# Alibi attention stacks: one 72-row transfer each for queries and keys, with the bf16 parts stored singly

## What is computed

```python
q = (x @ Wq + bq).reshape(Bb, Ss, H, HD)      # H = 16, HD = 8
k = (x @ Wk + bk).reshape(Bb, Ss, H, HD)
v = (x @ Wv + bv).reshape(Bb, Ss, H, HD)
scores = jnp.einsum('bthd,bshd->bhts', q, k) / jnp.sqrt(jnp.asarray(HD, x.dtype))
alibi = _alibi_bias(Ss, Ss, x.dtype)          # slope of the head times -|k - q|
scores = scores + alibi[None]
scores = jnp.where(causal[None, None], -jnp.inf, scores)
attn = jax.nn.softmax(scores, axis=-1)
out = jnp.einsum('bhts,bshd->bthd', attn, v).reshape(Bb, Ss, Dd)
return out @ Wo + bo
```

## Time and profile before

| | |
|---|---|
| median of the runs | 1447.83 us |
| the profiled execution | 1447.86 us |
| its span, first to last instruction | 1446.1 us |
| PE busy | 1324.8 us, 92% |
| DVE busy | 1028.3 us, 71% |
| ACT busy | 754.1 us, 52% |
| POOL busy | 379.0 us, 26% |
| block C, first to last score matmul | 718.2 to 999.7 us |
| DMA data moved | 34.17 MB |

### The profile page before, as it was taken

How to read it: one execution, slowest core, us unless ns; L and a number is a source line. 1 busy time by engine, 2 the same in 40 slices (tenths; PEclk the granted TensorE clock), 3 DMA queues, 4 the chain that set the end, 5 groups by cost and what they waited for, 6 DMA issues and landing times.

```text
span 1446.1 us, 23967 instructions
## 1 busy us (share of the span) xinstructions
PE 1324.8 (92%) x9009; PEld 791.1 (55%) x9009; DVE 1028.3 (71%) x2201; ACT 754.1 (52%) x1617; POOL 379.0 (26%) x304
## 2 busy tenths in 40 slices
PE   6999999999999999999768999999889989899986
PEld 4777676767677766333222333334356765367652
DVE  5767776676857684776657676767578885898855
ACT  3545444444534443434224666666667874388851
POOL 0000000001000001334550000001458881498822
PEclk9999999999999999999866999999999999999998
DMA  5000000000000000000202321110011110011101
GB/s 147 1 1 0 1 1 1 1 1 1 1 1 1 1 1 0 1 1 0 96 19 81 90 80 39 39 37 2 23 27 31 31 32 8 4 39 31 31 15 30
DMA packets 28686, 34.17 MB, mean 24 GB/s; under 512 B 6594, under 2 KB 21132, under 8 KB 27276
## 3 DMA queue, kind: packets, MB, share of 16 engines
q1 hardware_dynamic: 28572, 32.64, 8.3%
HBM read 20.11 MB, written 4.39 MB: 17 GB/s over the span
## 4 chain that ended last, share of the span: by engine, by line
PE 74%; DVE 13%; ACT 4%; issue 3%; POOL 3%; DMA 2%; SPq 0%; POOLq 0%; DVEq 0%; ACTq 0%
PE ps L695 13%; PE ps L715 8%; PE ps L730 7%; PE ps L1067 5%; PE ps L1026 4%; PE ps L1047 3%; PE ps L1124 3%; DVE negmax L1459 2%; PE ps L904 2%; PE ps L898 2%; PE ps L666 2%; PE ps L1167 2%; PE ps L1250 2%; PE ps L1189 2%; PE ps L1221 2%
## 5 line engine op out<-in xcount | busy, mean ns | idle before, releaser
L2281 ACT ACTIVATE probsT<-ps 128x512 f32<-128x512 f32 (+1 forms) x304 | 163.8, 577 | 107.4 <-PE ps L1051 95.1
L1459 DVE TENSOR_REDUCE negmax<-ps 128x1 f32<-128x1024 f32 x128 | 150.7, 1219 | 72.6 <-PE ps L715 72.5
L2103 ACT ACTIVATE probs<-ps,negmax 128x1024 f32<-128x1024 f32 x128 | 142.5, 1114 | 80.6 <-DVE negmax L1459 76.7
L2456 POOL TENSOR_SCALAR rstd<-mv 128x4 f32<-128x4 f32 (+1 forms) x31 | 7.2, 232 | 595.9 <-DVE mv L1394 595.6
L2109 ACT COPY probsT<-ps 128x512 f32<-128x512 f32 x128 | 74.8, 584 | 168.2 <-PE ps L730 168.1
L730 PEld LDWEIGHTS ps<-ident,probs 128*128 128x128 f32 x1024 | 114.5, 141 | 66.3 <-issue 44.1
L730 PE MATMUL ps<-ident,probs 128*128 128x128 f32 x1024 | 138.2, 277 | 6.6 <-DVE probsT L1472 3.4
L1026 PE MATMUL ps<-arena 76*128 76x512 bf16 (+3 forms) x384 | 113.6, 355 | 26.6 <-DVE cmax L1727 20.8
L715 PE MATMUL ps<-k_st,q_st 64*128 64x512 f32 x512 | 128.8, 622 | 5.9 <-ACT probs L2103 5.9
L1727 DVE CUSTOM_DVE_ANT_0 k_st<-ps,rel 128x256 f32<-128x256 f32 (+7 forms) x128 | 96.8, 756 | 44.2 <-PE ps L1026 43.3
L1727 DVE CUSTOM_DVE_ANT_0 q_st<-ps,rel 128x256 f32<-128x256 f32 (+7 forms) x128 | 96.7, 756 | 42.0 <-PE ps L1026 41.2
(11 more groups left out here) (233 smaller groups left out, 2543.9 us busy)
## 6 DMA issues: line engine op xcount, KB each, us to landing
probsT<-probsT SPq DMA_DIRECT2D x62, 128.0 KB, 2.4
arena<-c_parts SPq DMA_DIRECT2D x32, 192.0 KB
arena<-c_parts SPq DMA_DIRECT2D x16, 128.0 KB
arena<-in_L_ffn_w_dram SPq DMA_DIRECT2D x3, 512.0 KB
c_parts<-probsT SPq DMA_DIRECT2D x2, 768.0 KB, 3.5
arena<-in_c_far_dram SPq DMA_DIRECT2D x16, 96.0 KB
c_parts<-work SPq DMA_DIRECT2D x2, 768.0 KB, 11.1
work<-in_L_ffn_wqkv_dram SPq DMA_DIRECT2D x1, 1536.0 KB, 11.9
```

What stands on the lines that cost most here:

```text
L1459: dve.tensor_reduce(negmax[:, u:u + 1], s2, AX_X, ALU.max, negate=True).then_inc(s_a_negmax, 1)
L2103: act.activation(probs[:, u % NPB, :], s2, ACT.Exp, bias=negmax[:, u:u + 1], accum_out=rowsum[:, u:u + 1]).then_inc(s_a_exp, 1)
L2281: act.activation(c_p[:, kt % 2, j0:j0 + heads, q0 - kt * P:q0 - kt * P + n], ps[:, 4 + c % 2, 0:heads * n].rearrange("p (h n) -> p h n", n ...
```

## The change

- The parts of queries and keys get a DRAM tensor each: `q_scr` of shape (batch, group, 3 parts, 32 rows, 1024) and `k_scr` of shape (batch, group, 5 slots, 32 rows, 1024), where slots 3 and 4 repeat parts 0 and 1.
- Each part is stored as soon as it is there, queries and keys apart: eight transfers of 256 KB per batch (3 for queries, 5 for keys) in place of two of 768 KB. The DRAM side of each starts with the 4 groups.
- A stack has nine products (also q2 with k2): its middle part is 72 rows on either side, and each side comes in one transfer. `SHALLOW` becomes 84 and `DEEP` 87.
- The constants of a stack (`c_far`) are a function of their own. For sequences 0 and 1 they are loaded once the weights of block B have been turned (`s_fp`), ahead of the stores; for the others they stay where they were, ahead of `c_stack`.
- PE waits for 5 transfers per stack (`STACK`) and not 9.

```diff
-SHALLOW = FAR + 64
+SHALLOW = FAR + 72
...
-        scr = nc.dram_tensor("c_parts", (2, 3, BATCH, P, SEQ), BF16, kind="Internal").ap()
+        q_scr = nc.dram_tensor("c_q_parts", (BATCH, GROUPS, 3, STRIP, SEQ), BF16, kind="Internal").ap()
+        k_scr = nc.dram_tensor("c_k_parts", (BATCH, GROUPS, 5, STRIP, SEQ), BF16, kind="Internal").ap()
...
-        STACK = 16 * 9
+        STACK = 16 * 5
...
-            def c_store(b):
-
-                for w in range(2):
-                    sp.wait_ge(s_c_r2, 2 * b + w + 1)
-                    sp.dma_start(scr[w, :, b, :, :].rearrange("n p c -> p n c"), c_part[b][:, w, :, :])\
-                      .then_inc(s_c_scr, 16)
+            def c_store(b, part):
+
+                sp.dma_start(q_scr[b, :, part], c_part[b][:, 0, part, :]).then_inc(s_c_scr, 16)
+
+            def c_store_keys(b, part):
+
+                for slot in range(part, 5, 3):
+                    sp.dma_start(k_scr[b, :, slot], c_part[b][:, 1, part, :]).then_inc(s_c_scr, 16)
+
+            def c_stores(b):
+
+                for part, done in enumerate((s_c_p0, s_c_p1, s_c_r2)):
+                    sp.wait_ge(done, 2 * b + 1)
+                    c_store(b, part)
+                    sp.wait_ge(done, 2 * b + 2)
+                    c_store_keys(b, part)
+                sp.wait_ge(s_c_scr, 16 * 8 * (b + 1))
...
+            def c_stack(s):
+
+                g, b, buf = s % GROUPS, s // GROUPS, s % 3
+                n = 4 * SEQ
+                q = q_scr[b, g].rearrange("t (e j) n -> (t e) (j n)", j=4)
+                k = k_scr[b, g].rearrange("t (e j) n -> (t e) (j n)", j=4)
+                k = bass.AP(k.tensor, k.offset, [[HD1 * n, 3], [n, 3 * HD1], [1, n]])
+                sp.dma_start(c_q2[buf][FAR:SHALLOW, :, :].rearrange("p j n -> p (j n)"),
+                             q.unsqueeze(0).to_broadcast([3, 3 * HD1, n])).then_inc(s_c_stack[buf], 16)
+                sp.dma_start(c_k2[buf][FAR:SHALLOW, :, :].rearrange("p j n -> p (j n)"), k)                  .then_inc(s_c_stack[buf], 16)
+
+            sp.wait_ge(s_fp, 9)
+            c_far(0)
+            c_far(1)
+            c_stores(0)
             c_stack(0)
             c_stack(1)
...
                 if s == 0:
                     sp.wait_ge(s_e_x2, UNITS_B)
+                    c_far(2)
                     c_stack(2)
-                    c_store(1)
-                    sp.wait_ge(s_c_scr, 64)
+                    c_stores(1)
                 if 1 <= s and s + 2 < SEQS:
                     sp.wait_ge(s_c_turned, NPARTS * s)
+                    c_far(s + 2)
                     c_stack(s + 2)
```

More of the change, by code:

```diff
@@ L513, in c_stack, with c_far @@
+            def c_far(s):
+                g, buf = s % GROUPS, s % 3
+                sp.dma_start(c_q2[buf][0:FAR, :, :].bitcast(U16), a["c_far"][0, g, 0:FAR]).then_inc(s_c_stack[buf], 16)
+                sp.dma_start(c_k2[buf][0:FAR, :, :].bitcast(U16), a["c_far"][1, g, 0:FAR]).then_inc(s_c_stack[buf], 16)
+                sp.dma_start(c_k2[buf][SHALLOW:DEEP, :, :].bitcast(U16), a["c_far"][1, g, FAR:FAR + 3])                  .then_inc(s_c_stack[buf], 16)
             def c_stack(s):
                 g, b, buf = s % GROUPS, s // GROUPS, s % 3
-                heads = slice(4 * HD1 * g, 4 * HD1 * (g + 1))
@@ L517, in c_stack @@
[L517 to L528, removed]
@@ L530, in _ @@
-            c_store(0)
-            sp.wait_ge(s_c_scr, 32)
+                n = 4 * SEQ
[4 more added lines that the diff above has]
+                             q.unsqueeze(0).to_broadcast([3, 3 * HD1, n])).then_inc(s_c_stack[buf], 16)
```

## The result

| kernel | median us | runs | against before |
|---|---|---|---|
| before | 1449.32 | 5 | |
| changed | 1456.85 (1451.99 to 1459.02) | 5 | 1.0051, interval 1.0036 to 1.0065 |

The change makes the kernel 0.5% slower, 7.5 us by the medians. The profiled execution of the changed kernel took 1451.99 us, the shortest of its runs, with a span of 1450.2 us. So its trace shows the mechanism, and less than the usual loss: the five runs have mean granted clocks of 0.962 (1451.99 us) down to 0.958 (1459.02 us), in the order of their times.

The account below looks back on a forecast made before the run. PE was taken as the bound, busy 92% of the span, with 1.0 us directly recoverable from faster stacks. Terms 0.9 + 2.7 - 0.7 + 2.2 = 5.1 us on 1447.86 gave 1453.0 us, range 1446.5 to 1458.

Parts of the forecast that it names:

- Batch 0: First stack, held until batch 0's stores land: lands 723.2 us, wanted at 722.3; cost 0.9 us, between 0 and 2.0.
- Batch 1: Maxima of s = 1, written after batch 1's stores land: PE waits for them, cost 2.7 us.
- The clock: Behind PE's wait for the maxima of s = 1: granted clock falls to 0.50, cost 2.2 us.
- Stack 3: Stack of s = 3 lands 1.5 us later, PE 2.7 later: the 1.0 us wait at 831.45 goes, -0.7 net.
- the 8 us that the prediction weighs as an alternative: Stack of s = 3: by the skill's coalescing rule, four transfers saved bring it up to 8 us earlier, returning 1.0 us.
- Rival 1: Both waits, for stack 0 and the maxima of s = 1, but clock holds: +2.9, 1450.8 us; chance 0.20.
- Rival 2: Stores not on four engines, or starting beside the stack: nothing waits at the maxima of s = 1, 1447.1 us; chance 0.20.
- Rival 3: Stores slower than the row rate: 28 us per batch, 6.4 us more in each, about 1462 us; chance 0.08.
- Rival 4: Full clock for part of 757 to 783 us: up to 11 us back, 1444.7 or about 1442 us; chance 0.08.
- Ninth product ... 84 and 87 rows: nothing.: PE's score and turned matmuls: 379 ns whatever the number of rows, so the ninth product's extra rows cost nothing.

Follow-up runs that it names:

- wide_b0: Changed kernel with only batch 0's stores split by group into four of 32 rows: 1451.1 us, ratio 1.0021.
- wide_b1: Changed kernel with only batch 1's stores split by group into four of 32 rows: 1449.7 us, ratio 1.0012.
- after_again: The changed kernel run once more, nothing altered: 1457.5 us, ratio 1.0058 against the kernel before.
- wide_both: Changed kernel with each store of both batches split by group into four of 32 rows: 1444.2 us, ratio 0.9966.
- swap: Changed kernel with stack transfers reading DRAM with 24 rows outermost, three repetitions inside; stores left as they were: 1444.7 us, ratio 0.9967.
- pad_rows: far_only plus eight rows of zeros in each stack, loaded once per buffer (84 and 87 rows): 1442.9 us, ratio 0.9969.
- far_only: Kernel before with only the constants of s = 0 and 1 loaded early, ahead of the stores: 1447.7 us, ratio 1.0001.
- narrow_only: Kernel before with the changed kernel's eight narrow stores per batch and nothing else: 1454.2 us, ratio 1.0042.
- wait_late: Changed kernel with SP's wait for batch 1's stores moved behind the issue of the stack of s = 3: 1454.2 us, ratio 1.0038.

## Where the prediction held and where it did not

**The direction and the mechanism of the loss held.** I forecast 1453.0 us, slower, within 1446.5 to 1458; measured 1456.85. I was not sure of it: with a bound of 0.3%, I gave slower 0.45 and same 0.48, and by the terms named there same is 0.55 (0.147 + 0.16 + 0.20 + 0.04). The step on which all of it rests, that a store that starts with 4 on one side gets four engines, was right: share 0.26 and 101 GB/s for 0.25 and 97. By the Trainium skill's rule on the number of engines ("DMA: Bandwidth & Descriptors", section "Why a DMA increments its semaphore by 16 and not by 1") it had to be 4; the trace agrees, and with 3 and 12 for the stacks as well.

**Batch 0.** Stack 0's first transfer left at 705.60 (forecast 705.7) and PE began at 723.54 (forecast 723.2). But block B ended 1.6 us earlier in this execution, with PE's turn of yT at 713.50 and not 715.10, so the same landing cost more: 2.05 us at DVE for 0.9. (That mark lies anywhere from 713.5 to 717.0 us in the fourteen profiles.) And the step "cost 0.9 us, between 0 and 2.0" left out the clock: by wide_b0 and wide_b1 batch 0's stores cost 5.5 to 6.4 us.

**Batch 1.** The maxima left at 808.09 (forecast 807.7 and the shift before it) and PE stood 3.07 us for 2.7, 4.80 in the second profile. The landing took 2.6 us (809.56 to 812.2) and not 1.5.

**The clock** is the term that was mis-sized: "take 2.2". It fell as forecast, but for ten microseconds (0.52 from 812 to 822) and in after_again from 815 to 825, not three to six. Wait and clock together cost 6.9 to 7.8 us where I had 2.7 + 2.2. Over all runs the clock has the larger part: the missing share times the span is 60.2 us on average in after_again and 48.6 in wide_both, 11.6 us for a difference of 13.3. (This is an estimate from above, since it also counts the lower clock while PE stands.)

**Stack 3.** The 1.0 us wait is gone, as forecast, and because PE is late, as forecast: in wide_both, where it is not, PE stands 0.92 us for this stack. So merging six transfers into two let PE stand no more than 0.1 us less; the 8 us that the prediction weighs as an alternative are not there. Rival 1 (the clock holds) fell in both profiles of the changed kernel. Rival 2 (the stores are harmless) fell for the changed kernel; its place was right, though: swap is the case in which the stack no longer stands ahead of them. Its time, 1447.1, was wrong by 2.4 us: swap has 1444.7. Rival 3 (slower stores) fell, at 101 GB/s; its own terms, 6.4 us twice on top of the forecast, give 1465.8 us and not 1462. Rival 4 (the clock comes back earlier) fell for the changed kernel, which is at 0.50 from 758 to 784 us as the kernel before; in wide_both and swap, though, the lower clock ends 16 us behind M0, where it is 18.5 us in the kernel before: the way to which I gave 0.08.

**The step that failed most is "Ninth product ... 84 and 87 rows: nothing."** The durations did not change, 379 ns as read from the earlier trace rows:

```profile
L1042 PE MATMUL ps<-arena x384: 216/379/634, 723.5 to 1006.8; 84*128 84x512 bf16 x144, 84*128 84x128 bf16 x16, 84*128 84x256 bf16 x16, 84*128 84x384 bf16 x16
```

But by pad_rows eight more rows take 4.8 us off, most of it through the clock. That the forecast was near is luck, because two errors cancelled: the stores cost 13.3 us (after_again less wide_both) where I had 5.8 for both waits and the clock, and the rest of the change gained about 5 us where I had 0.7.

**What stays open**: why more rows bring the clock back earlier, why they do not with a late first stack, and in which stretches some 3 of the 4.8 us are; what makes the clock fall once more at 750 us in the kernel before and in none of the others whose first stack is in time, and why far_only, without this fall, is no faster; and the 3 us between narrow_only and the changed kernel, whose intervals overlap.

## What to carry to other kernels

Look at the outermost dimension of both sides of a transfer before its size: cutting a store into groups of 4 took twelve of its sixteen engines away, and the two lines that put 24 in front of 3 gave a stack four times as many, which merging six transfers into two had not. Narrow transfers share the same few engines: with a stack on three and stores on four both queued, the share from 770 to 785 us was 0.22 in the changed kernel, that of four engines and not of seven. So what stands behind them there is late even if SP is free; find the smallest transfer that somebody waits for, and ask what is queued ahead of it. And a wait of 3 to 5 us in a stage bound by PE cost about twice its length here, 6.9 to 7.8 us, where the clock fell with it.

## What the runs showed of the hardware that I had not expected

- Eight rows of zeros more in the contraction (84 for 76, 87 for 79), at the same 379 ns per matmul, took 4.8 us off the kernel (1447.7 to 1442.9), with the granted clock back at its upper level 16 us and not 19 us behind the maxima of s = 0. With a late first stack, 84 rows had 18 to 19 us all the same. pad_rows has the lowest median of the study, 0.31% under the kernel before (interval 0.20 to 0.42%), with the products of the kernel before; wide_both, at 0.34%, can't be told from it.
- SP can stand in an issue: 12.71 us for two stores of 256 KB, 12.62 us at a later load, each time with much queued ahead of them. In swap, where the stack ahead takes twelve engines, two stores still took 10.41 us, so the stack on three engines is not the only reason.
- A small transfer of 24 KB took 6.9 us from issue to report behind stores that kept four engines busy (wait_late), and 1.5 us in the kernel before.
- Kernels that wait spread wider: 7.0 to 8.2 us from the shortest to the longest run in the changed kernel (both times), wide_b0, wait_late and narrow_only, 6.0 in wide_b1, 2.5 to 5.0 in the seven others, and 6.5 us over 31 runs of the kernel before.
